# Graph network kernel, one core: the degree flag taken behind all maxima on VectorE, and layer-1 accumulators that walk through seven PSUM banks

## The reference

```
# network A: layer norm, two attention layers, a dense product
for layer (4 heads of 192 features, then 2 heads of 96):
    h = x @ W                                # per head
    e = leaky_relu(s_src[src] + s_dst[dst])  # one score per edge, head and self loop
    ee = exp(e - max over the edges of dst)
    out = sum(ee * h[src]) / sum(ee)         # per dst
x = layernorm(x + concat(x, out2) @ Wu + bu)
# network B: two graph convolutions
deg = edges per dst (with the self loop); dinv = 1 / sqrt(deg)
h = relu(dinv * (C.T @ (dinv * (x @ W1))) + b1)      # C: edge counts
x = layernorm(x + dinv * (C.T @ (dinv * (h @ W2))) + b2)
```

## Time and profile before

| what | value |
|---|---|
| three runs | 892.07, 895.50, 897.51 us |
| median | 895.5 us |
| profiled execution, its own time | 891.93 us |
| its span | 890.2 us |
| mean granted TensorE clock | 0.959 |
| PE busy | 805.7 us (91%) |
| DVE busy | 612.3 us (69%) |
| ACT busy | 287.3 us (32%) |

### The profile page before, as it was taken

How to read it: one execution, slowest core, us unless ns; L and a number is a source line. 1 busy time by engine, 2 the same in 40 slices (tenths; PEclk the granted TensorE clock), 3 DMA queues, 4 the chain that set the end, 5 groups by cost and what they waited for, 6 DMA issues and landing times.

```text
span 890.2 us, 12683 instructions
## 1 busy us (share of the span) xinstructions
PE 805.7 (91%) x4306; PEld 667.0 (75%) x4307; DVE 612.3 (69%) x1304; ACT 287.3 (32%) x523; POOL 18.7 (2%) x32
## 2 busy tenths in 40 slices
PE   4999999998899199999989879699998999999997
PEld 3845555655666099999955679478887888999997
DVE  1788888887738999999689799765641823212444
ACT  4334555543532143434232444322221411111000
POOL 3100000000000040000000000000000000000000
PEclk9999999999989699999989898799999999999999
DMA  8300000000000040110000400000003000000111
GB/s 290 138 1 1 1 0 0 0 0 1 1 0 1 7 172 1 60 60 1 1 1 0 134 1 1 2 1 1 1 0 126 1 1 1 1 1 1 54 71 50
DMA packets 9573, 26.34 MB, mean 30 GB/s; under 512 B 623, under 2 KB 2477, under 8 KB 9138
## 3 DMA queue, kind: packets, MB, share of 16 engines
q1 hardware_dynamic: 9522, 25.65, 8.3%
HBM read 21.78 MB, written 3.87 MB: 29 GB/s over the span
## 4 chain that ended last, share of the span: by engine, by line
PE 66%; DVE 19%; issue 5%; DVEq 5%; ACT 3%; DMA 1%; SPq 0%
PE ps L1059 63%; DVE scrap L510 5%; DVE att L662 3%; DVEq L319 3%; DVE att L626 3%; DVE ohs_abc L521 1%; DMA w<-in_L_gnn_W 1%; DVEq L521 1%; DVE ohd_ab L524 1%; DVE ohd_c L524 1%; PE ps L1198 1%; DVE xohd L524 1%; DVE out L649 1%; DVE gw1lo L702 1%; PE ps L1339 1%
## 5 line engine op out<-in xcount | busy, mean ns | idle before, releaser
L1059 PE MATMUL ps<-g,att 128*128 128x193 f32 x800 | 133.2, 330 | 19.8 <-DVE att L626 19.8
L1059 PEld LDWEIGHTS ps<-g,att 128*128 128x128 f32 x800 | 132.3, 192 | 20.8 <-issue 20.4
L931 ACT ACTIVATE att<-att,ssrc 128x1250 f32<-128x1250 f32 x60 | 80.2, 1338 | 116.1 <-DVE att L662 116.0
L626 DVE SCALAR_TENSOR_TENSOR att<-att,ct 128x1250 f32<-128x1250 f32 x60 | 88.0, 1467 | 4.8 <-ACT att L931 4.6
L662 DVE SCALAR_TENSOR_TENSOR att<-uB,s 128x1250 f32<-128x1250 f32 x60 | 91.1, 1522 | 0.0
L1059 PE MATMUL ps<-wp,xT 128*128 128x388 f32 x240 | 87.6, 503 | 0.9 <-ACT xT L878 0.6
L1059 PE MATMUL ps<-yhi,ctr 128*128 128x384 f32 x200 | 67.7, 339 | 0.0
L726 DVE SCALAR_TENSOR_TENSOR ylo_a<-ps,dinv,yhi 128x384 fp32r<-128x384 f32 x32 | 19.0, 615 | 61.9 <-ACT yhi L815 61.9
L1059 PEld LDWEIGHTS ps<-wp,xT 128*128 128x128 f32 x240 | 42.8, 191 | 24.6 <-issue 1.0
L1059 PE MATMUL ps<-h2x,att 128*128 128x97 f32 x400 | 51.8, 294 | 10.0 <-DVE out L649 4.6
L1059 PEld LDWEIGHTS ps<-h2x,att 128*128 128x128 f32 x400 | 50.4, 209 | 11.4 <-DVE att L626 8.0
(11 more groups left out here) (238 smaller groups left out, 1467.2 us busy)
## 6 DMA issues: line engine op xcount, KB each, us to landing
wux<-in_L_gnn_Wu SPq DMA_DIRECT2D x2, 2304.0 KB, 15.9
gw<-in_L_gnn_W SPq DMA_DIRECT2D x2, 2304.0 KB, 10.0
uB<-u_dram SPq DMA_DIRECT2D x3, 1280.0 KB, 5.9
xs<-in_x SPq DMA_DIRECT2D x1, 3456.0 KB
out<-ybuf SPq DMA_DIRECT2D x9, 384.0 KB, 2.3
w<-in_L_gnn_W SPq DMA_DIRECT2D x1, 2304.0 KB, 8.5
w2x<-in_L_gnn_W SPq DMA_DIRECT2D x1, 576.0 KB, 9.2
wuo<-in_L_gnn_Wu SPq DMA_DIRECT2D x1, 576.0 KB
```

The lines of the kernel that those rows point to most:

```text
L626: v.scalar_tensor_tensor(a, a, HUGE, ct[:, q, 0:N], ALU.min, ALU.mult).then_inc(att_ready, 1)
L931: a.activation(at_, at_, ACT.Exp, bias=ssrc[:, h, q:q + 1]).then_inc(att_exp, 1)
L1059: return t.matmul(o, lhsT, rhs, start=start, stop=stop, **kw)
```

## The change

On VectorE the three `maxima` calls of heads 1 to 3 move from behind `dinv2` to ahead of the wait for TensorE's transpose of `degmax`. For the heads of layer 1 the bank is no longer b but the entry (5 hp + b) mod 7 of the list 0, 1, 2, 3, 4, 6, 7: head 0 uses 0, 1, 2, 3, 4; head 1 uses 6, 7, 0, 1, 2; head 2 uses 3, 4, 6, 7, 0; head 3 uses 1, 2, 3, 4, 6. TensorE waits at the first matmul into a bank for the release of the accumulator seven places earlier, where it waited for that five places earlier. Bank 5 stays with the small transposes. Heads 4 and 5 (layer 2) keep banks 0 to 4 and the old wait.

```diff
+        def acc_bank(hp, b):
+            return (0, 1, 2, 3, 4, 6, 7)[(5 * hp + b) % 7] if hp < H1 else b
...
             v.tensor_reduce(degmax[:, :], deg[:, :], AX.X, ALU.max).then_inc(dmax_ready, 1)
+            for h in range(1, H1):
+                maxima(h)
             v.wait_ge(dmax_ps, 1)
             vstep(v.tensor_reduce(zz[0:1, 0:1], ps[0:1, 5, 0:P], AX.X, ALU.max))
             v.tensor_scalar(wide[0:1, 0:1], zz[0:1, 0:1], float(EXACT), None, ALU.is_gt).then_inc(wide_ready, 1)
             v.wait_ge(sq_ready, 1)
             vstep(v.reciprocal(dinv[:, :], sqd[:, :]))
             v.tensor_tensor(dinv2[:, :], dinv[:, :], dinv[:, :], ALU.mult).then_inc(dinv_ready, 1)
-            for h in range(1, H1):
-                maxima(h)
             v.wait_ge(x_added, 2 * X2)
...
-                    acc = ps[:, b, 0:2 * wid].rearrange("p (t n) -> p t n", t=2)
+                    acc = ps[:, acc_bank(hp, b), 0:2 * wid].rearrange("p (t n) -> p t n", t=2)
...
-                        if q == 0 and half == 0 and hp > 0:
+                        if q == 0 and half == 0 and hp >= H1:
                             t.wait_ge(acc_out, 5 * (hp - 1) + b + 1)
+                        elif q == 0 and half == 0 and 5 * hp + b >= 7:
+                            t.wait_ge(acc_out, 5 * hp + b - 6)
...
-                        last = mm(ps[:, b, half * wid:(half + 1) * wid], att[:, n % NA, dt_ * P:(dt_ + 1) * P], rhs,
+                        last = mm(ps[:, acc_bank(hp, b), half * wid:(half + 1) * wid], att[:, n % NA, dt_ * P:(dt_ + 1) * P], rhs,
```

## The result

| what | before | after |
|---|---|---|
| median of the runs | 893.79 us (4 runs, 891.24 to 897.51) | 877.54 us (4 runs, 876.44 to 879.47) |
| ratio, 95% interval | | 0.9831, 0.9806 to 0.9856 |
| profiled execution, its span | 890.2 us | 877.7 us |
| TensorE idle ahead of layer 1 | 19.78 us | 5.63 us |

The change is 1.7% faster, 15.1 us of 893.8 by the ratio (12.9 to 17.3 by its interval); the medians lie 16.3 us apart. The profiled execution of the changed kernel is the slowest of its four (879.47 us), so the spans differ by only 12.5 us. The forecast was 881.4 us with a range of 877.5 to 886.5, and a gain of 14.1 us.

A forecast was written before the change was run, and what follows sets the result against it. VectorE and TensorE waiting for each other in turn was taken as the bound. Profiled execution: 891.93 - 14.2 - 0.2 = 877.5; against the 895.5 median 881.1, with 0.3 taken back 881.4 us, range 877.5 to 886.5.

The forecast's parts named there:

- Stage: Ahead of layer 1: VectorE's 14.49 us wait for TensorE's transpose comes back as TensorE's later wait for VectorE.
- Maxima: VectorE's 30 maxima, moved into the wait, take 48.69 us as before, 243.3 to 292.0; upper bound +1.3 us if slower.
- The next thing that is late: Ahead of the first scores: VectorE waits 0.16 us for the x tiles, whose last copy ends at 292.96.
- ScalarE's table load: Ahead of the first exponential: the load ends at 294.26, 0.24 us before the first scores, and costs nothing.
- TensorE: Start of layer 1: first product 4.91 us behind first scores, idle 5.6 us, half-speed restart as before; term -14.2 us.
- rival of a shorter half-speed stretch: TensorE's restart ahead of layer 1 has less or no half speed; gain up to 15.8 us, 879.7 us; chance 0.10.
- the bound of 1.4 us for what could be kept: Layer 1: without half speed TensorE arrives 1.8 us earlier; with seven banks 1.4 us of it could be kept.
- Transfers: SyncE's transfers and GpSimd's additions move forward 15 us, attention 14.2, so same tiles of head 0; nothing gained or lost.
- Banks: Layer 1: seven banks remove a 0.18 us wait of TensorE at the second head boundary; term -0.2 us.
- rivals of no change: The wait is hidden elsewhere, the x tiles ending later than 292.96; time 887 to 895.5 us; chance 0.09.
- of dearer matmuls: Layer 1's matmuls pay for the walk through the banks: slower above 18 ns more a record; chance 0.03.
- a change that doesn't do what it says: VectorE still waits for TensorE's transpose behind the maxima; no chance of its own given.

The follow-up runs named there:

- e1: Kernel before with only the maxima of heads 1 to 3 moved ahead of the flag, banks 0 to 4: 877.37 us against 892.52, ratio 0.9825.
- e3: Kernel before with only the maxima of head 1 moved ahead of the flag, banks 0 to 4: 878.11 us against 892.52, ratio 0.9831.
- e7: Kernel before with TensorE's transpose of degmax and ScalarE's square root moved earlier, VectorE's order kept: 885.36 us against 892.04, ratio 0.9923.
- e2: Kernel before with only the seven banks and their waits, maxima where they were: 892.34 us against 892.52, ratio 1.0002.
- e0: The changed kernel measured again, against the kernel before: 877.90 us against 892.04, ratio 0.9832.
- e4: Changed kernel plus 40 small identity matmuls on TensorE ahead of layer 1, seven banks: 879.84 us, ratio 0.9851 to the kernel before.
- e5: Changed kernel plus 40 small identity matmuls on TensorE ahead of layer 1, but banks 0 to 4: 879.79 us, ratio 0.9853 to the kernel before.
- e8: Changed kernel plus 22 small identity matmuls on TensorE ahead of layer 1, seven banks: 874.74 us against 894.53 for the kernel before, ratio 0.9792.
- e9: Changed kernel plus 22 small identity matmuls ahead of layer 1, but banks 0 to 4: 879.97 us against 894.53 for the kernel before, ratio 0.9837.
- e11: Changed kernel plus 22 small identity matmuls, seven banks, run again beside the changed kernel on one chip: 874.75 us, ratio 0.9804 to the kernel before.
- e10: The changed kernel run again, beside the version with 22 small matmuls on one chip: 878.78 us, ratio 0.9851 to the kernel before.
- e6: Kernel before with only TensorE's transpose of degmax moved ahead of the last source rows: 891.76 us against 892.52, ratio 0.9996.

## Why the prediction was right

**Stage.** Right: the wait of the earlier trace rows was paid back one for one ahead of layer 1. `e1`, `e3` and `e7`, which take away all or half of it, and `e2`, which leaves it, each came as this says.

**Maxima.** 48.30 us instead of 48.69; the bound of +1.3 us was not needed.

**The next thing that is late.** Right in what it is, mis-sized in how much. The forecast had 0.16 us of waiting for the x tiles, read off one execution. Of the ten profiled executions with maxima moved ahead of the flag nine show a wait: 1.82 us in the changed kernel, 0.74 (`e0`), 1.11 (`e1`), 2.17 (`e3`), 1.13 (`e4`), 0.85 (`e5`), 0.67 (`e8`), 2.00 (`e9`) and 0.86 (`e11`); `e10` shows none. The three long ones are the three executions that were late at `degmax`. VectorE takes 49.2 us from the start of `degmax` to the end of `dinv2` in the changed kernel, and the same in `e0` and `e10`. What varies is when ScalarE has copied the last x tile: 50.9 us behind `degmax` in the changed kernel, 49.8 in `e0` and 48.7 in `e10`. In the kernel before this variation was free, because VectorE was 14 us late for the tiles. In `e0`, which reaches `degmax` when the kernel before did (243.03 and 243.12), the first scores come 50.03 us behind it instead of 64.19: 14.2 us gained, as forecast. In the profiled execution of the changed kernel the later x tiles took 1.1 us off that. So the x tiles now set the start of layer 1, and work taken off VectorE ahead of them would bring nothing more.

**ScalarE's table load.** Right at nothing: the exponential had 0.33 us to spare.

**TensorE.** The first product came 4.91 us behind the first scores (301.88 - 296.97), as said, and the idle time was 5.63 (said: 5.6). The clock fell as said, and the half-speed stretch lasted 4.1 us instead of 3.6, 0.24 us of it in the rows. The rival of a shorter half-speed stretch did not come by itself. `e8` brought it about, and the bound of 1.4 us for what could be kept was nearly what it gave (1.29, from 138.16 to 136.87).

**Transfers.** Right that nothing is lost. GpSimd's additions begin 4.9 us behind the first product (306.82) and not 7.6 us behind it as before (319.85), so not beside quite the same tiles, and the layer takes the same time.

**Banks.** Right that they are worth next to nothing in the time. That the 0.18 us at the second boundary is theirs is true only where TensorE starts the layer as quickly as before: with five banks that stretch takes 33.00 and 32.95 us in `e6` and `e7` (first two tiles in 8.55 and 8.59), but 32.83 in `e1` and `e3` (8.95 and 8.80). With the first two tiles at 8.78, as in the profiled execution of the changed kernel, these two say that five banks would have done as well. The second bound, that the banks matter only when TensorE gets ahead, is shown by `e8` against `e9`.

**The total.** The forecast gain of 14.1 us lies within the measured 12.9 to 17.3. The absolute time came out 3.9 us lower than said: 1.7 us of that is the kernel before, whose median over four runs is 893.79 and not 895.5. The other 2.2 us are no more than what the stages vary by that hold the same instructions in all kernels. Behind layer 1 there are 444.8 us before and 442.6 after, but between 442.3 and 446.1 in the profiled executions of the experiments; ahead of `degmax` there are between 242.9 and 246.6. The median of 877.54 us lies only just above the lower end of the stated range, 877.5: that it didn't fall below it is luck, the gain is not. The 0.3 us that the forecast took back for the dearer bounds went the wrong way. Whether the earlier start moves the clock's changes to better places behind layer 1, or this is chance, the runs do not settle.

The rivals of no change, of dearer matmuls and of a change that doesn't do what it says are refuted by the time, by 164 ns a record in `e2`, and by the missing wait ahead of the flag.

## What to carry to other kernels

A wait on one engine in the middle of two that hand work to each other is read twice in the table of stretches: once where it stands, once as the other engine's idle time later. Work that is ready and has no part in the wait is put ahead of it, and only as much as the wait is long. Before what is waited for is brought forward instead, look for a second wait right behind it, as the one for the square root was here: the profile shows a wait only where the engine stood still, and this one was over while the engine stood in the first. And a buffer that gives an engine room to run ahead is worth something only if that engine gets ahead; find out what holds it back first, here the half-speed restart. And once the wait is gone, ask what sets the start of the stage now: here it was the x tiles, by 0.7 to 2.2 us in nine executions of ten.

## What the runs showed of the hardware that was not expected

A float32 matmul of the 128 x 128 identity took 0.227 us at full clock (80 records, 9.09 us, for 40), where I had counted half of it. And 5.07 us of such matmuls, with 0.72 us of idle time behind them, kept the granted clock at full (2.4 GHz) from TensorE's last x tile into layer 1 in `e8`, `e9` and `e11`. Without them, 5.63 us of idle time let it fall to half (1.2 GHz) 2.9 us behind TensorE's stop. The first 40 records took 6.77 us instead of 8.78.
